# An attention-and-FFN kernel on one core: a new order for its opening, filler products on TensorE, and statistics moved to every second tile

## The reference, cut to what matters

```
xn  = layernorm(x)                         # per token
q1  = (clip(round(xn  / s1 + z1), 0, 255) - z1) * s1
q2  = (clip(round(ctx / s2 + z2), 0, 255) - z2) * s2
x   = x + q1 @ q2                          # 2 x (1024 x 2048) @ (2048 x 2048)
xn2 = layernorm(x)
x   = x + xn2 @ W.T + bias + routed_lora(xn2)   # top 2 of 8 experts, rank 16
```

## Time and profile before

| | |
|---|---|
| median of 3 runs | 1009.53 us (1008.64 to 1012.52) |
| the profiled execution's own time | 1009.48 us |
| its span in the trace | 1007.8 us |
| PE busy | 966.3 us, 96% of the span |
| DVE busy | 780.7 us, 77% |
| ACT busy | 433.9 us, 43% |
| POOL busy | 133.6 us, 13% |
| PE L1623, the chunks | 232.8 us, 1536 products; 12.1 us idle before them |

### The profile page before, as it was taken

The page is one execution under the profiler, slowest core; times in us unless marked ns, Lnnn a source line. Parts: engine busy times, 40 slices in busy tenths (PEclk is TensorE's granted clock), DMA queues, the critical chain, the costliest instruction groups (busy, mean ns, idle before and its releaser), DMA issues.

```text
span 1007.8 us, 15099 instructions
## 1 busy us (share of the span) xinstructions
PE 966.3 (96%) x5875; PEld 524.8 (52%) x5875; DVE 780.7 (77%) x1430; ACT 433.9 (43%) x468; POOL 133.6 (13%) x168
## 2 busy tenths in 40 slices
PE   1699999999999999999999999999999999999998
PEld 1466666666689644444444444444444444444444
DVE  7778877687645769986887677866788798798885
ACT  4687778566642256444443334212223223322310
POOL 2416354446200000000000000000000000000000
PEclk9899999999999999999999999999999999999999
DMA  9847668588642256864676564248643143232320
GB/s 376 354 155 284 253 249 284 205 328 315 207 134 70 92 183 189 283 234 154 201 235 196 178 237 154 69 141 289 206 142 125 69 152 113 81 136 78 111 74 31
DMA packets 62311, 185.65 MB, mean 184 GB/s; under 512 B 6896, under 2 KB 19488, under 8 KB 56096
## 3 DMA queue, kind: packets, MB, share of 16 engines
q1 hardware_dynamic: 58648, 174.18, 48.5%
q10 hardware_dynamic: 2312, 8.39, 2.1%
q0 software_dynamic: 1280, 2.12, 2.0%
HBM read 151.07 MB, written 33.60 MB: 183 GB/s over the span
## 4 chain that ended last, share of the span: by engine, by line
PE 78%; DVE 3%; DMA 2%; ACT 1%; issue 0%; DVEq 0%; ACTq 0%
PE pair L1768 31%; PE pair L1791 28%; PE pair L1623 13%; PE pair L1747 4%; PE pair L1737 1%; DMA spread<-scratch 1%; DMA scratch<-w_max 1%; DMA w_r<-in_w_n 1%; PE pair L1803 1%; DVE w_p L1187 0%; ACT w_r L774 0%; PE pair L1713 0%; PE pair L1638 0%; DVE cent L1243 0%; DVE cent L1282 0%
## 5 line engine op out<-in xcount | busy, mean ns | idle before, releaser
L1768 PE MATMUL pair<-x2p,w_p 128*128 128x512 f16 x1536 | 336.7, 379 | 0.2 <-DVE w_p L1187 0.2
L1768 PEld LDWEIGHTS pair<-x2p,w_p 128*128 128x128 f16 x1536 | 150.2, 98 | 181.1 <-DVE w_p L1187 0.7
L1623 PE MATMUL pair<-q1T,ctx_q 128*128 128x342 f16 x1536 | 232.8, 312 | 12.1 <-DVE xt L977 5.7
L1623 PEld LDWEIGHTS pair<-q1T,ctx_q 128*128 128x128 f16 x1536 | 149.4, 98 | 89.8 <-issue 10.7
L1791 PE MATMUL pair<-x2p,w_slot 128*128 128x512 f16 x744 | 163.8, 379 | 0.0
L801 ACT ACTIVATE sq<-pair,lsc 128x512 f32<-128x512 f32 x64 | 43.7, 682 | 236.7 <-PE pair L1747 200.8
L1567 POOL TENSOR_SCALAR ctx_u<-ctx_f,par 128x512 uint8<-128x512 f32 x128 | 114.9, 911 | 148.2 <-DMA ctx_f<-in_ctx 91.8
L1791 PEld LDWEIGHTS pair<-x2p,w_slot 128*128 128x128 f16 x744 | 72.9, 98 | 87.7
L829 ACT ACTIVATE w_slot<-w_q,usc 128x1024 f16<-128x1024 f32 x32 | 36.5, 1146 | 92.1 <-DVE usc L1402 27.2
L1791 PE MATMUL pair<-x2p,x2p 128*128 128x512 f16 x336 | 74.3, 379 | 0.0
L977 DVE SCALAR_TENSOR_TENSOR xt<-pair,par,xt 128x342 f32<-128x342 f32 (+1 forms) x96 | 53.7, 565 | 16.0 <-PE pair L1623 15.6
(11 more groups left out here) (214 smaller groups left out, 1078.4 us busy)
## 6 DMA issues: line engine op xcount, KB each, us to landing
ctx_f<-in_ctx SPq DMA_DIRECT2D x32, 1024.0 KB, 7.2
xt<-in_xT SPq DMA_DIRECT2D x32, 512.0 KB, 4.5
w_r<-in_w_n SPq DMA_DIRECT2D x32, 512.0 KB, 7.0
w_f<-in_w_t SPq DMA_DIRECT2D x32, 512.0 KB, 5.5
w_q<-in_w_t SPq DMA_DIRECT2D x32, 512.0 KB, 5.1
outT<-u SPq DMA_DIRECT2D x63, 256.0 KB, 3.4
rows<-in_x SPq DMA_DIRECT2D x15, 1024.0 KB, 9.2
x_kept<-xt ACTq DMA_DIRECT2D x16, 512.0 KB, 4.8
```

Source lines behind the costliest of these rows:

```text
L1623: ins = M.matmul(bank[at % RING][:, 0:W3], ctx_q[n % NQ][:, k, :], q1T[b][:, k, c * W3:(c + 1) * W3], start=(k == 0), stop=(k == KT - 1))
L1768: M.matmul(base_bank(m)[:, :], w_p[j % 2][wh][:, k, :], x2p[0][:, k, xh, t], start=(k == 0 and q == 0), stop=(k == KT - 1 and q == 2))
```

## The change

- `STATS_AT`, `SCALE_AT`, `STD_AT`, `BYTES_AT`, `LOAD_AT`: each entry is moved so that statistics stand at even n, scales at odd n. The entry for T = 12 keeps its statistics at 6, while its load goes from 6 to 7.
- `ON_ACT`: ScalarE converts context tile 1 and the even ones from 4 on.
- ScalarE's opening: copy 6 goes ahead of bytes 7, copy 7 ahead of bytes 8.
- VectorE's opening: context tile 2, then the scale of group 3, both ahead of take-back (1,0). Context tile 4 is no longer converted there (it is ScalarE's now), and 5 is converted at n = 3.
- TensorE's opening: 24 products of ones with ones (128 columns) into a bank that nothing else uses at that time, between row sum 1 and chunk (0,0); chunk (1,1) goes ahead of turn 7, row sum 6 and the turn of the bound. The last turn (row tile 15) with the row sum before it is written out between chunks (17,0) and (16,1).

```diff
-STATS_AT = {3: 11, 6: 12, 7: 13, 9: 14, 11: 15}
-SCALE_AT = {4: 6, 8: 7, 12: 8}
-STD_AT = {3: 6, 7: 7, 11: 8}
-BYTES_AT = {3: 10, 5: 11, 7: 12, 9: 13, 11: 14, 13: 15}
-LOAD_AT = {6: 12, 8: 13, 10: 14, 12: 15}
-
-ON_ACT = [1] + list(range(5, STEPS, 2))
+STATS_AT = {4: 11, 6: 12, 8: 13, 10: 14, 12: 15}
+SCALE_AT = {5: 6, 9: 7, 13: 8}
+STD_AT = {4: 6, 8: 7, 12: 8}
+BYTES_AT = {4: 10, 6: 11, 8: 12, 10: 13, 12: 14, 14: 15}
+LOAD_AT = {7: 12, 9: 13, 11: 14, 13: 15}
+
+ON_ACT = [1] + list(range(4, STEPS, 2))
...
             ln_std_of(4)
+            ln_copy(6)
             ln_bytes_of(7)
-            ln_copy(6)
+            ln_copy(7)
             ln_bytes_of(TT)
-            ln_copy(7)
             ln_std_of(5)
...
             take_y(0, 0)
+            ctx_ready_of(2)
+            ln_scale_of(3)
             take_y(1, 0)
-            ln_scale_of(3)
-            ctx_ready_of(2)
             ln_stats_of(7)
...
             acc_of(0)
-            ctx_ready_of(4)
             lo_of(1)
...
                     take_y(n - 1, 2)
+                    ctx_ready_of(n + 2)
                     take_y(n, 2)
...
+            def keep_busy(count):
+                for _ in range(count):
+                    M.matmul(bank[5][:, 0:P], ones16[:, :], ones16[:, :], start=True, stop=True)
+
             turn(0)
             turn(1)
             row_sum(0)
             turn(2)
             row_sum(1)
+            keep_busy(24)
             chunk(0, 0)
...
             chunk(0, 1)
+            chunk(1, 1)
             turn(7)
             row_sum(6)
             turn_bound(0)
-            chunk(1, 1)
             chunk(2, 1)
...
                     chunk(n, 0)
                     chunk(n + 1, 0)
+                    row_sum(ROWS - 2)
+                    turn(ROWS - 1)
                     chunk(n, 1)
                     continue
```

## The result

| | before | changed |
|---|---|---|
| median, 5 runs each | 1009.74 us (1008.64 to 1012.52) | 1013.87 us (1013.21 to 1016.35) |
| ratio | | 1.0042, 95% interval 1.0022 to 1.0062 |
| span of the profiled execution | 1007.8 us | 1013.1 us |

The measured time lies above the range given, and beyond rival D too (1011.6). D named the right place, the loop, and priced its rounds at +5.4, more than the +4.1 they measured against before; what it lacked, the later start and the slow clock behind the handover, is in the table further down.

What follows compares the result with a forecast made beforehand. TensorE bounds from 182 us, the VectorE/ScalarE loop before. Opening -5.6, loop start 3.6 earlier, rounds +1.3, then a 1.3 us copy wait put the handover 2.0 earlier: 1009.48 to 1007.5 us, range 1003.9 to 1010.8.

Steps and rivals of the forecast that it cites:

- rival D: VectorE/ScalarE loop: rounds with statistics, a conversion and a scale lengthen, rounds +5.4 us, kernel 1011.6 us; chance 0.13.
- the twelve rounds: Loop from take-back (3,2) to take-back (15,2), tiles 4 to 15: 94.8 us forecast against 93.48 before.
- Parts 1 and 2: TensorE's opening: filler warms the first chunk (1.7 us), context tile 2 and copies come earlier; chunk (0,2) 5.6 us earlier.
- Part 3: ScalarE's string before the loop, with context tile 4 in it: third column add at 70.6, loop starts 3.6 us earlier.
- Part 4: Moved statistics in the loop: tile 12's +2.0 us, tile 13's -0.7, others unchanged; rounds 94.8 us, +1.3.
- The lower bound of the rounds: Loop: -4.6 us if every round of statistics were as the cheapest of its kind.
- Its signs of being wrong: VectorE waiting for TensorE between 80 and 165 us, or the loop's rounds under 92 us.
- Part 5: Handover at 182 us: TensorE waits 1.3 us for the last copy; turn of the bound at 178.4 against 180.35, -2.0 us.
- Rival C: Opening's gain carried whole to the end: 1003.9 us, or 998.2 with all 5.7 us of TensorE's stalls gone; chance 0.2.

Runs made afterwards that it cites:

- after_no_filler: The changed kernel without the 24 filler products; ratio 1.0063 to the kernel before.
- opening_bytes8: opening_only with ScalarE's conversion of row tile 8 put back ahead of copy 7; ratio 0.9960 to the kernel before.
- ctx4_on_dve: The changed kernel with context tile 4 converted by VectorE as before; ratio 1.0023 to the kernel before.
- load_early: The changed kernel with LOAD_AT one tile earlier for row tiles 12 to 15, statistics left where the change put them; ratio 0.9976 to the kernel before.
- copy15_first: The changed kernel with the copy of row tile 15 ahead of the conversion of context tile 18 on ScalarE; ratio 1.0013 to the kernel before.
- tables_only: The kernel before with only the five tables, ON_ACT, context tiles 4 and 5 and the last turn changed; ratio 1.0090, 9.1 us slower.
- opening_only: The changed kernel with tables, ON_ACT, context tile 4 and last turn put back; filler, opening orders and copies stay; ratio 0.9975, 2.5 us faster.

## Why the prediction was wrong, point by point

| step | forecast | measured |
|---|---|---|
| chunk (0,2) starts | 54.9 | 55.39 |
| third column add | 70.6 | 73.12 |
| take-back (3,2) | 75.9 | 78.69 |
| the twelve rounds | 94.8 | 97.57 |
| turn of the bound | 178.4 | 183.99 |
| wait ahead of it | 1.3 | 1.20 |
| chunks (16,2) and (17,2) | 4.6 | 6.3 |

**Parts 1 and 2 held**, filler, third context tile, copies, to 0.5 us at chunk (0,2); after_no_filler shows the filler's share. The prediction expected the filler to warm the first chunk in some executions and not in others; it did so in all nine that were profiled.

**Part 3 failed by 2.8 us.** The step that failed is the string of ScalarE, taken over from the kernel before as "12.0 us with no gap", starting 1.7 us behind chunk (0,2). Its rows in the changed kernel, root of group 5, conversion of row tile 9, second column add, second square and third column add:

```profile
56.17 0.19 ACT L671 ACTIVATE std<-lnt 128x1 f32<-128x1 f32 x1
57.80 2.10 ACT L680 ACTIVATE q1u<-rows,lnt 128x2048 uint8<-128x2048 f32 x1 [1.44 <-DVE lnt L929]
...
65.55 1.15 ACT L703 ACTIVATE xt<-xt,colt 128x1024 f32<-128x1024 f32 x1 [0.64 <-DVE xt L977]
...
68.42 1.03 ACT L719 ACTIVATE pair<-xt 128x1024 f32<-128x1024 f32 x1 [0.54 <-DVE acc L993]
...
73.12 1.14 ACT L703 ACTIVATE xt<-xt,colt 128x1024 f32<-128x1024 f32 x1
```

It starts 2.4 us behind (0,2), 0.7 later than forecast, since the root and with it the scale of row tile 9 now stand behind the conversion of row tile 8. And it has two gaps, 1.2 us together, in which it waits for VectorE, which is late by its own wait of 2.33 us for row tile 10. The prediction said that "the next row load on SP's queue ... is not later". That is true: it was issued at 56.29, before at 56.30. But its statistics now came 5 us earlier. The question "what is late next" was put to the load's start and not to its reader. The rest is the 0.5 of Part 2 and small differences. opening_bytes8 takes both terms away at once: the string starts 1.7 us behind (0,2) (56.08 and 54.39) and has no gap. The conversion of context tile 4 in ScalarE's string, priced at 1.99, measured 1.9 at the end (ctx4_on_dve).

**Part 4 failed by 2.8 us.** The mechanism was the right one, the size was not, and the term that was mis-sized is the wait for rows. The round with row tile 12's statistics was priced at 9.50 and took 10.0 (wait 1.89, not 1.36). That with row tile 13's was given 10.8, with its wait of 0.73 gone; it took 12.2, with a wait of 1.43. Those with 14's and 15's took 9.8 and 12.7 (waits 1.63 and 1.92), where 9.50 and 12.39 had been carried over with 1.36 and 1.60 in them. That with 11's took 10.2, against 9.92, without a wait. So the sum held 4.3 us of waiting for rows and the kernel had 6.9, which is 2.5 of the 2.8. A wait for a transfer was carried over as if it belonged to the round; it belongs to the queue, and load_early took 7.1 us off the rounds by the queue alone. The lower bound of the rounds, -4.6, still left the cheapest round with its wait in it, so the range had no room for what the loads could give. Two of the marks that the prediction set were missed here, a sum of the rounds of 94 to 96 and no wait before row tile 13's statistics. Its signs of being wrong stayed silent, because both guarded against a faster loop only.

**Part 5** foresaw the new wait within 0.1 us and put what it does to the clock at nothing, although a slow chunk behind an idle stretch stood in the earlier trace rows. copy15_first shows it in the trace: without the 1.2 us of wait the pair takes 4.6 us again, 1.7 less. Part 5 also closed with "no idle TensorE to lose or gain" behind the handover. Between the kernel before and the changed kernel that held: 821.0 and 820.9 us from the end of the pair to the end of the span. Over all thirteen profiles this stretch is 820.9 to 825.0 us long, with the wait before 390 us among what varies. Whether that goes with the kernel or with the execution is not shown.

Sum: -2.0 forecast, +2.8 for the start, +2.8 for the rounds, +1.7 for the clock is +5.3, the difference of the spans. The medians give 4.1; the slow stretches of the clock differ between executions, and single runs of the changed kernel spread over 3 us. The 9.1 of tables_only is of the size that its trace shows, a turn of the bound 7.9 later and a pair 1.7 slower. Its cost and the opening's gain sum to 9.1 - 2.5 = 6.6 against the measured 4.2. The intervals of the two overlap (about 5.0 to 8.2, and 2.2 to 6.2), so the times do not show that the halves fail to add. In the single traces they miss by 2.6 us at the end of the pair. The rounds of tables_only are 1.1 us longer than the changed kernel's. In opening_only, TensorE needs 8.9 us from take-back (15,2) to the turn of the bound, 1.5 more than before, behind the slow chunk at 149.95.

**Rival C** was wrong as a forecast for this change and right that TensorE's stalls could be had: with conversions moved to the even tiles and the statistics left at odd ones, TensorE's stalls go almost wholly. The prediction took the new spacing of the statistics for even and did not ask on which parity they stood relative to the conversions.

## What to carry to other kernels

Where two engines pass work round a loop, an extra piece can cost nothing in the place where its engine waits for the other, and its full length next to another extra piece: put statistics and conversions in different rounds, not in the same one. When a step is brought forward, follow the transfers that it reads as closely as the engines, and look at what is issued ahead of them in the queue. A short new wait of TensorE can have a second price in the clock behind it; here it had one ahead of one-column products, and between full chunks only in one execution.

## What the runs showed of the hardware that was not expected

- A wait of 1.2 us, followed by the column sums (1.8 us of one-column products), was enough for the next 32 products of 342 columns to take 6.3 us from start to start instead of 4.6 (granted clock 0.50 in 186 to 188 us). All five kernels with that wait show it, with 6.3 to 7.5 us; none of the eight without it does (4.6 in each), though they have the same column sums. The wait by itself was not enough: before the chunk at 153.10 in the earlier trace rows TensorE waited 1.78 us, and the changed kernel waited up to 1.77 us in its loop, and the chunks behind took the fast 2.48. That it is the one-column products which make the difference is an inference; no run here takes them away. Between full chunks, waits of 2.02 and 2.00 us slowed the next ones in the profiled execution of opening_only, and one of 1.99 us in opening_bytes8 did not (2.48).
- 24 products of ones in a 3 us gap made the next chunk take 2.48 us instead of 3.9 to 4.7, with 0.44 us of idle time between them (up to 3.06 in other executions).
- A 1 MB transfer issued right behind 1.5 MB of others took a median of 9.0 us to land, and 5.4 us when issued right ahead of them, while the context and x tiles went from 6.9 and 4.4 us to 8.2 and 5.9.
